# Extra TensorE products ahead of each query product and behind the slot table of a two-layer transformer kernel

## The reference, cut to what matters

```python
q = jnp.einsum('bth,hd->btd', inputs, WQ)
k = jnp.einsum('bth,hd->btd', inputs, WK)
v = jnp.einsum('bth,hd->btd', inputs, WV)
score = jnp.einsum('bqd,bkd->bqk', q, k) / scale
score = score * local[None, :, :]            # a band of 64 around the diagonal
attn = jax.nn.softmax(score, axis=-1)
return jnp.einsum('bqk,bkd->bqd', attn, v)
...
logits = jnp.einsum('bsd,de->bse', tensor, Wr) + br
probs = jax.nn.softmax(logits, axis=-1)
topv, topi = jax.lax.top_k(probs, NUM_SELECTED)     # 2 of 16 experts
h = jax.nn.relu(jnp.einsum('bsd,edh->bseh', tensor, W1) + b1)
y = jnp.einsum('bseh,ehm->bsem', h, W2) + b2
out = jnp.einsum('bse,bsem->bsm', gate, y)
```

## Time and profile before

| | |
|---|---|
| median of 3 runs | 616.4 us (612.55 to 616.71) |
| the profiled execution's own time | 614.65 us |
| its span, first to last instruction | 612.9 us |
| TensorE (PE) busy | 479.8 us, 78% |
| VectorE (DVE) busy | 388.9 us, 63% |
| ScalarE (ACT) busy | 276.5 us, 45% |
| GpSimd (POOL) busy | 260.9 us, 43% |
| mean granted TensorE clock | 0.855 of 2.4 GHz |

### The profile page before, as it was taken

One profiled execution on the slowest core, in us unless ns is written; L12 is line 12 of the kernel. 1 busy time (PEld: TensorE's weight loads), 2 busy tenths in 40 slices (PEclk: granted clock), 3 DMA queues, 4 the chain that ended last, 5 costly groups with the idle time before them and its releaser, 6 DMA issues.

```text
span 612.9 us, 11004 instructions
## 1 busy us (share of the span) xinstructions
PE 479.8 (78%) x2424; PEld 335.3 (55%) x2424; DVE 388.9 (63%) x1260; ACT 276.5 (45%) x748; POOL 260.9 (43%) x362
## 2 busy tenths in 40 slices
PE   3589998329999999279897797798576789899950
PEld 3467776207777777136554464464352456677640
DVE  3535777604555555359999999999934544555535
ACT  1445554104444444166775675585323115455520
POOL 2110366621444444425354584473457201555550
PEclk9965555558999999689999999898958997899985
DMA  7998611252221110372330510000002020222106
GB/s 241 336 382 280 113 37 35 64 89 58 54 57 50 48 40 19 103 193 61 85 87 10 133 48 5 15 18 2 17 23 83 24 64 12 61 78 73 51 7 205
DMA packets 57517, 51.52 MB, mean 84 GB/s; under 512 B 8653, under 2 KB 50110, under 8 KB 57075
## 3 DMA queue, kind: packets, MB, share of 16 engines
q1 hardware_dynamic: 51250, 41.85, 24.8%
q0 software_dynamic: 5056, 8.48, 4.4%
q10 hardware_dynamic: 1152, 0.53, 0.6%
HBM read 37.19 MB, written 15.60 MB: 86 GB/s over the span
## 4 chain that ended last, share of the span: by engine, by line
PE 46%; DVE 26%; issue 12%; DMA 5%; POOL 4%; ACT 2%; SPq 1%; another core or an unknown queue 1%; DVEq 0%; POOLq 0%; ACTq 0%
PE bank L1369 13%; PE bank L1384 6%; DVE qk_sums L1117 5%; PE bank L1461 4%; PE bank L1377 3%; PE bank L1523 3%; PE bank L1415 2%; POOL sorted_tokens L464 2%; DVE work L1154 2%; DVE work L1110 2%; DMA sorted_tokens<-rows,router_at 2%; PE bank L1515 2%; PE bank L1362 2%; DVE router_dx L344 2%; DVE big L1110 2%
## 5 line engine op out<-in xcount | busy, mean ns | idle before, releaser
L712 POOL DMA_INDIRECT results<-work x94 | 92.0, 979 | 150.2 <-DVE work L1087 76.3
L1073 DVE TENSOR_TENSOR work<-bank,bias_big 128x512 f32<-128x512 f32 (+1 forms) x94 | 57.2, 608 | 102.9 <-PE bank L1369 94.2
L1369 PE MATMUL bank<-big,work 128*128 x188 | 93.9, 583 | 8.3 <-ACT work L821 8.1
L1415 PE MATMUL bank<-Wqkvb,work 128*128 128x512 f32 x192 | 96.6, 632 | 2.6 <-ACT work L837 2.4
L821 ACT ACTIVATE work<-bank,mcol 128x128 f32<-128x128 f32 x94 | 43.0, 458 | 122.9 <-PE bank L1362 110.1
L1415 PEld LDWEIGHTS bank<-Wqkvb,work 128*128 128x128 f32 x192 | 34.5, 198 | 31.7 <-issue 27.8
L1384 PE MATMUL bank<-big,work 128*128 x376 | 49.6, 275 | 0.0
L1384 PEld LDWEIGHTS bank<-big,work 128*128 128x128 f32 x376 | 45.7, 192 | 0.1
L1369 PEld LDWEIGHTS bank<-big,work 128*128 128x128 f32 x188 | 29.8, 200 | 17.9 <-issue 17.8
L464 POOL DMA_INDIRECT sorted_tokens<-rows,router_at x32 | 31.5, 985 | 13.6 <-issue 13.4
L753 POOL DMA_INDIRECT sorted_tokens<-rows,router_at x32 | 31.5, 983 | 13.4 <-issue 7.7
(11 more groups left out here) (222 smaller groups left out, 1107.8 us busy)
## 6 DMA issues: line engine op xcount, KB each, us to landing
work<-sorted_tokens SPq DMA_DIRECT2D x94, 65.0 KB
big<-in_w SPq DMA_DIRECT2D x48, 88.0 KB
big<-in_W SPq DMA_DIRECT2D x1, 4096.0 KB, 16.4
bias_big<-in_b SPq DMA_DIRECT2D x1, 4096.0 KB, 33.1
big<-results SPq DMA_DIRECT2D x16, 256.0 KB, 2.9
sorted_tokens<-zeros SPq DMA_DIRECT2D x2, 975.0 KB
sorted_tokens<-zeros SPq DMA_DIRECT2D x24, 65.0 KB
Wqkvb<-in_WqkvbT SPq DMA_DIRECT2D x1, 1544.0 KB
```

The costliest lines, as they stand in the source:

```text
L712: pool.indirect_dma_start(ys[l], bass.IndirectOffsetOnAxis(xg[b][:, D:D + 1].bitcast(I32), 0), yo[b], None, bounds_check=TOPK * T - 1, oob ...
L1073: dve.tensor_tensor(hb[b % 2][:, 0:width], bank[:, 1 + b % 2, 0:width], bias_big[:, bass.ds(e * width, width)], ALU.add).then_inc(e_hb, 1)
L1369: pe.matmul(bank[:, 1 + b % 2, 0:width], xgT[b % 2], w[:, bass.ds(e * width, width)], start=True, stop=True).then_inc(e_h, 1)
L1415: last = pe.matmul(bank[:, 2 * k + i, :], h3T[b], Wqkvb[:, k * HD + i * 512:k * HD + (i + 1) * 512], start=True, stop=True)
```

## The change

A function `occupy(bk, n)` is added. It issues n products of 512 columns (weights `Wa[:, 0, :]`, moving operand the first 512 columns of `hT` behind the margin) into PSUM bank `bk`, with no semaphore of their own. Nobody reads them. `query` calls it with n = 2 for the bank that its own product then overwrites in part, and behind `turn_slots(0)` it is called once with n = 14 for bank 0. Nothing else is altered. All lines below the first hunk have a number higher by 6.

```diff
@@ -1293,8 +1293,14 @@
             pe.wait_ge(a_v, NT + 1)
             pe.wait_ge(ld_router, 64)
 
+            def occupy(bk, n):
+
+                for _ in range(n):
+                    pe.matmul(bank[:, bk, :], Wa[:, 0, :], hT[:, BAND:BAND + 512], start=True, stop=True)
+
             def query(t, b, q):
                 after(pe, b_qT, t - 1)
+                occupy(ends[b % 2], 2)
                 pe.matmul(bank[:, ends[b % 2], 0:P], Wa[:, 0, :], hT[:, bass.ds(t * P + BAND, P)],
                           start=True, stop=True).then_inc(b_q, 1)
 
@@ -1351,6 +1357,7 @@
             count_experts(0)
             cumulate_tiles(0)
             turn_slots(0)
+            occupy(0, 14)
             pe.wait_ge(t_ready, 1)
 
             experts = table(mybir.EngineType.PE, tbl, P, E - 1)
```

## The result

The changed kernel takes 627.15 us (median of 4 runs, 625.36 to 632.15) against 616.56 us (612.55 to 617.79) beside it: 1.0196 times the time before, 95% interval 1.012 to 1.0273. The ratio is that of the means, 627.95 and 615.86. That is 12 us slower, 7 to 17 by the interval; the medians are 10.6 us apart. The profiled execution has a span of 623.6 us, 10.7 above the one before.

The account below looks back on a forecast made before the run. TensorE at 1.2 GHz was taken to pace the attention loop, later nearly even with GpSimd. Profiled 614.65 + 3.8 (loop) + 0.7 (fourteen) = 619.2 us; with 1.75 to the median, 621 us, range 614 to 629.

Parts of the forecast that it names:

- the loop's own bounds: Attention loop: total shift +3.8 us, bounds 0 (steps 0.3 us shorter) to +9 (steps 0.3 us longer).
- What one extra product costs: Each 512-column fp32 product: 0.86 us at the high clock, 1.72 at the low, weight loads hidden beside the product ahead.
- the loads show: Rival: 46 products each show two weight loads, adding 10 us, 631 us in all; chance 0.08.
- Does the clock rise: TensorE's clock: high from 44.34 us until the last query, then low again soon after.
- The clock does not hold: Rival: clock falls in each of five rank steps, 629 us; never rising, 670 us; chance 0.17 together.
- The start of the loop, +4.7 us: First attention-loop steps, to the score called eighth: at 66.5 us instead of 61.86, as TensorE had little to do there.
- The step of 3.46: Attention-loop step without rank: own work halved to 1.74 us plus two products, 1.72, gives 3.46 us.
- The middle, +0.1 us: Attention loop from there to the last score: five steps of 4.73 and four of 3.46, 37.5 us against 37.38.
- The end, -1.0 us: After the last score: low clock, pace of before, but TensorE saves 0.92 us of waiting for GpSimd.
- GpSimd: GpSimd's 5.01 us hold before its first send won't return in full; first send at 72 to 74 us.
- The fourteen, +0.7 us: Behind the slot table: first slot 3.8 us late, first three slots gain 3.1; net +0.7, bounds -1.4 and +4.1.
- The rival that becomes faster: GpSimd sets the loop's end, and the high clock lasts so the fourteen start warm: 612 us; chance 0.13.

Follow-up runs that it names:

- four narrow ahead: Changed kernel with four products of 128 columns ahead of each query product instead of two of 512, fourteen kept; ratio to the kernel before 1.0018.
- Loop only: Changed kernel without the fourteen products behind the slot table, two ahead of each query product kept; ratio to the kernel before 1.0136.
- two behind rank: Changed kernel with the two products per step moved behind the query and rank products, fourteen kept; ratio to the kernel before 1.0111.
- four ahead: Changed kernel with four products of 512 columns ahead of each query product instead of two, fourteen kept; ratio to the kernel before 1.0597.
- one ahead: Changed kernel with one product of 512 columns ahead of each query product instead of two, fourteen kept; ratio to the kernel before 1.0003.
- ten: Changed kernel with no products in the attention loop and ten instead of fourteen behind the slot table; ratio to the kernel before 0.9966.
- slots only: Changed kernel without the products in the attention loop, only the fourteen behind the slot table; ratio to the kernel before 1.0020.
- one ahead and ten: Changed kernel with one product ahead of each query product instead of two, ten instead of fourteen behind the slot table; ratio to before 0.9970.

## Why the prediction was right or wrong

The forecast was 621 us with a range to 629; measured 627. The sign, the range and what the clock does in the loop were right. The size was off: +4.5 foretold, +12 by the ratio, +10.7 in the profiled spans, and a change of under 1% had been given 0.60. That 627 lies within 629 is in part luck, since that end of the range was put there for a clock that falls in the rank steps, which cost 1.7 us and not 8. What did happen is the far end of the loop's own bounds, +9 for steps 0.3 us longer. By steps:

- *What one extra product costs.* Right. 0.86 us at the high clock, with 0.1 of a load in the open per group and no more; the 92 rows of line 1299 are there. The rival "the loads show" is out (four narrow ahead).
- *Does the clock rise.* Right for the loop: 1.00 to 67 us, 0.96 then. It stayed at 1.00 until 117.0 us, 9 us behind the last query, and was low when the fourteen began. "The clock does not hold" happened once, for one pair of products, at 1.7 us; with a probability of 0.17 it had been given 8 us. It explains a sixth of the loss. Loop only had such a spell too, in the same step; two behind rank and four ahead had none in the loop (1.00 over 62 to 100 us).
- *The start of the loop, +4.7 us.* Measured +5.9, counted from the first product. (The score that the prediction calls the eighth is by count the seventh, and its fourth the third; the times are those of the right rows.) The first three scores came as foretold. The step of 3.46 was 3.77, four times: 1.2 us.
- *The middle, +0.1 us.* This step failed: +5.4 us. "At the high clock a step's own work halves" is wrong. The own work went from 3.48 to 2.05 us, not 1.74 (one ahead, less its product), and two products add 1.72, so a step is 3.77 and longer than before. Of the 0.31 us that are missing to the half, 0.24 lie between the score and the query's line: 1.93 us before (58.38 to 60.31 in the earlier trace rows), 1.20 now (59.76 to 60.96), where half is 0.96. Why the score and the two products of `attend` gain less than the rest no run settles. Against the forecast of 37.5 us the sum is this: the four plain steps of this stretch (3.62 to 3.68 us, and 5.31 with the low spell) give 0.7 us, the low spell 1.7. In a rank step 2.98 us ahead of the rank products were 3.25, and 1.75 behind them 1.72, so 0.24 us more in each of five, 1.2. The rest, 1.7 us, is nearly all in the rank steps of 5.83 and 5.51 us, in which VectorE took up the rank products late. Loop only has the same two steps long (5.80 and 5.75), so it is no chance of one run, and ScalarE took up its next copy within 0.1 us of VectorE in both (80.39 and 90.97 us in the changed kernel), so it is not VectorE's own work that was late. What held the two is open.
- *The end, -1.0 us.* Measured -1.9 (21.08 against 23.01 from the last score to the slot table). The sign is right. But the reason was a low clock and a GpSimd that is no longer late, and the clock was 1.00 for the first 7 us of it (0.66 in the mean); which of the two gave how much was not tested, and traces of the same program differ by as much in this stretch (22.03 us in ten, 22.75 in slots only).
- *GpSimd.* The argument was that its hold before the first send belongs to full DMA queues and won't come back whole. It was 3.24 us, where before it was 5.01, and the queues had been quiet for over 3 us when the rows were ready. So it did not come back whole, but most of it is there without full queues too, and the first send was at 75.99 and not at 72 to 74. It did no harm: the chain that ended last runs through TensorE and VectorE in the loop of the changed kernel.
- *The fourteen, +0.7 us.* Right in size: 0.0 in the changed kernel, +0.9 in slots only, both within what traces differ by. The first slot's 3.8 us of lateness was 2.65 and 3.6, the gain of the first three slots 3.1 was 2.7.
- *The rival that becomes faster* named two things that turned out true of other kernels: GpSimd bounds the loop as soon as TensorE is quicker (one ahead and ten), and a start at the high clock gains 2 to 3 us if the products end in time (ten). With two and fourteen neither applied.

The sum of the marks: 5.9 + 5.4 - 1.9 = 9.4 us at the slot table, and as much at the fourth slot. The first product of the loop began 0.45 us earlier than before (43.89 after 44.34), so the fourth slot is 8.8 us later in the profiled execution. The remaining 1.9 us of the profiled spans lie behind it, where the clock falls at other places in the two traces. That is less than single runs of one kernel differ by, and no cause for it was shown.

## What to carry to other kernels

Filling TensorE to raise its clock pays only with time in which it has nothing to do, and only as long as it ends in time: ten products in a gap of 10.4 us gained 2 us, fourteen did not. Nor is it certain to hold: with one ahead and ten, the clock fell again 1.7 us behind the first slot's transpose. Inside a loop that TensorE paces, the filling must be shorter than what the clock saves, 1.43 us a step here: one product of 512 columns brought the step from 3.48 to 2.91 us and two to 3.77. And before a faster step is bought, look who is next: here GpSimd's round of 7.5 us per pair of tiles took all that was left. Last, a faster clock does not halve a step: take its gain from a trace at that clock before weighing it against the filling.

## What the runs showed of the hardware that was not expected

- Doubling the clock from 1.2 to 2.4 GHz took a step of small fp32 products with their transposes from 3.48 to 2.05 us, a factor of 1.7 and not 2.
- One product of 512 columns ahead of each query was enough for the high clock in one ahead and ten, and so were four of 128: 1.00 from 62 us to 94, past the last scores at 92 and 93. In one ahead it fell for 6.8 us, in the changed kernel, with two, for 3.4 (82.8 to 86.3), in four ahead not at all. These traces are too few to say that the second product makes it firmer; it cost 0.86 us a step.
- In two behind rank, passes of 512 columns took 0.85 us (46 to 49.4 us) while the profile gives the granted clock as 1.00; elsewhere in these traces that is the time of a pass at 0.50. Here the record of the clock and the rows do not agree, and the rows are what the time is made of.
- The time before GpSimd's first indirect DMA, from the end of its copies into `rows`, was 3.2 to 6.4 us in the ten traces. In the six whose copies ended before 67 us, while the DMA queues were still full (quiet from 68 to 70 us on), it was 3.9 to 6.4 and the send came at 70.2 to 71.8 us; in the four with later copies it was 3.2 to 3.4, with the queues quiet. What it waits for in these 3.2 us stays open.
